# Order of VectorE in a fused attention and expert kernel: row-sum inverse and one lower half of k ahead of routing steps 7 to 12

## The reference

```python
x = x + _L0_conv_ref(_ln_c(x), mask, Wq, Wk, Wv, Wg, Wo, Wb)
#   bias = x@Wb ; sim = q.k*scale + bias ; attn = softmax(where(mask, sim, -1e9))
#   out = ((attn @ v) * sigmoid(x@Wg)) @ Wo        per row r, 160 queries x 160 keys
t = _to_tokens(x)
t = t + _L0_ffn_ref(_ln_t(t), router_w, router_b, expert_w, expert_b)
#   softmax(t@router_w + b) -> top 2 of 8, renormed ; sum of p_k * (t@expert_w[k] + expert_b[k])
```

## Time and profile before

| | |
|---|---|
| median of three runs | 909.1 us |
| profiled execution | 911.06 us |
| its span, first to last instruction | 909.2 us |
| TensorE matmul busy | 812.7 us, 89% |
| VectorE busy | 760.7 us, 84% |
| GpSimd busy | 641.0 us, 71% |
| ScalarE busy | 485.4 us, 53% |
| from 400 to 500 us | TensorE 96.31, VectorE 89.52, GpSimd 77.23, ScalarE 58.02 us of 100 |
| granted TensorE clock | 0.974 over the span, 1.00 from 400 to 500 us |

### The profile page before, as it was taken

One profiled execution on the slowest core, in us unless ns is written; L12 is line 12 of the kernel. 1 busy time (PEld: TensorE's weight loads), 2 busy tenths in 40 slices (PEclk: granted clock), 3 DMA queues, 4 the chain that ended last, 5 costly groups with the idle time before them and its releaser, 6 DMA issues.

```text
span 909.2 us, 40901 instructions
## 1 busy us (share of the span) xinstructions
PE 812.7 (89%) x15532; PEld 536.6 (59%) x15532; DVE 760.7 (84%) x1818; ACT 485.4 (53%) x1049; POOL 641.0 (71%) x1029
## 2 busy tenths in 40 slices
PE   1999678999999999999999999999999999999743
PEld 1898345656656566665666656666666666656421
DVE  8998445898898898988989989899888998898764
ACT  3886235555565555655456554555546555565410
POOL 6994002677777677776777767777677777777786
PEclk9999989999999999999999999999999999999975
DMA  4563000011110011001110011100101001100000
GB/s 126 192 197 134 19 18 25 25 31 54 39 32 30 29 50 36 29 29 34 45 36 29 29 39 40 36 29 29 45 34 36 29 29 50 36 23 25 17 14 16
DMA packets 32461, 40.82 MB, mean 45 GB/s; under 512 B 6288, under 2 KB 27280, under 8 KB 32400
## 3 DMA queue, kind: packets, MB, share of 16 engines
q1 hardware_dynamic: 31920, 39.95, 13.3%
q10 hardware_dynamic: 480, 0.02, 0.0%
HBM read 13.74 MB, written 6.55 MB: 22 GB/s over the span
## 4 chain that ended last, share of the span: by engine, by line
PE 36%; DVE 35%; issue 19%; POOL 7%; ACT 1%; DVEq 1%; DMA 0%; POOLq 0%; ACTq 0%
DVE negm L826 6%; PE psS L1113 6%; DVE rinv L842 5%; PE psS L1088 5%; DVE prod L944 3%; POOL ln_s L376 3%; PE ps_o L1170 3%; PE ps_x L1173 2%; PE ps_x L1170 2%; PE ps_o L1173 2%; DVE og L857 2%; DVE rt L906 2%; DVE q_lo L778 2%; POOL xn L379 2%; DVE ogu L849 2%
## 5 line engine op out<-in xcount | busy, mean ns | idle before, releaser
L429 POOL TENSOR_TENSOR add<-prod 128x256 f32<-128x256 f32 x160 | 116.5, 728 | 100.4 <-DVE prod L944 100.4
L826 DVE TENSOR_REDUCE negm<-psS 128x12 f16<-128x1920 f32 x80 | 146.0, 1825 | 12.8 <-PE psS L1098 7.9
L376 POOL TENSOR_TENSOR ln_s<-ln_s,half 128x5 f32<-128x5 f32 (+1 forms) x60 | 86.2, 1436 | 38.6 <-DVE ln_s L882 30.8
L434 POOL TENSOR_TENSOR add<-add 128x128 f32<-128x128 f32 x200 | 91.4, 457 | 0.1
L602 ACT ACTIVATE hl<-xn 128x320 f16<-128x320 f32 x40 | 18.8, 470 | 129.4 <-POOL xn L379 129.4
L546 ACT ACTIVATE pt_b<-psS 128x1920 f32<-128x1920 f32 x40 | 70.9, 1771 | 18.9 <-PE psS L1132 15.1
L411 POOL TENSOR_TENSOR rinv_lo<-rinv,rinv_hi 128x160 f16<-128x160 f32 x40 | 19.8, 496 | 83.8 <-ACT rinv_hi L577 83.8
L436 POOL TENSOR_TENSOR ymix<-add 128x64 f32<-128x64 f32 x200 | 64.4, 322 | 15.7
L1088 PE MATMUL psS<-bm,ident 128*128 128x480 f16 (+1 forms) x320 | 68.4, 336 | 7.0 <-ACT pt_a L546 3.1
L417 POOL TENSOR_TENSOR og_lo<-og,og_hi 128x320 f16<-128x320 f32 x80 | 61.8, 794 | 17.0 <-ACT og_hi L583 17.0
L1113 PE MATMUL psS<-bt_hi,ident 128*128 128x320 f16 (+1 forms) x320 | 68.5, 337 | 2.3 <-DVE negm L826 2.3
(11 more groups left out here) (279 smaller groups left out, 2979.5 us busy)
## 6 DMA issues: line engine op xcount, KB each, us to landing
xin<-in_x SPq DMA_DIRECT2D x20, 320.0 KB, 3.0
xs_all<-xs_pair SPq DMA_DIRECT2D x20, 320.0 KB, 2.5
xs_q<-xs_all SPq DMA_DIRECT2D x40, 160.0 KB, 2.1
xs_v<-xs_all SPq DMA_DIRECT2D x40, 160.0 KB, 2.1
xin<-in_x SPq DMA_DIRECT2D x40, 160.0 KB, 2.2
out<-res SPq DMA_DIRECT2D x40, 160.0 KB, 1.8
w_raw<-in_expert_w SPq DMA_DIRECT2D x2, 128.0 KB
eb_raw<-in_expert_b SPq DMA_DIRECT2D x15, 2.0 KB
```

The costliest lines, as they stand in the source:

```text
L376: pool.tensor_tensor(ln_s[a][:, 3, 0:w], ln_s[a][:, 2, 0:w], half[:, 0:w], ALU.pow).then_inc(own, 1)
L429: pool.tensor_tensor(add1[t % 2][:], prod_of(t)[:, 0:4, :], prod_of(t)[:, 4:8, :], ALU.add).then_inc(mix_step[t], 1)
L434: pool.tensor_tensor(add2[t % 2][:], add1[t % 2][:, 0:2, :], add1[t % 2][:, 2:4, :], ALU.add).then_inc(mix_step[t], 1)
L826: dve.tensor_reduce(negm[c][:, :, 0:slots], psS[:, :, 0:slots * N].rearrange("i h (s j) -> i h s j", s=slots), AX.X, ALU.max, negate=True) ...
```

## The change

In VectorE's step `invert(n)` moves from behind routing step 9 to behind step 6, and `qk_low(n+2, a, 1, 1, ps_o)` from behind step 12 to right behind `invert`. The third group of routing steps (7 to 9) and the fourth (10 to 12) follow both. On SyncE the hand-written walk over the steps becomes `run_steps` with a new helper that leaves out the loads of the first steps.

```diff
+        def third_on(g):
+
+            return on(g) and not (isinstance(g, int) and g < 2)
...
             def step(n, a):
                 b = 1 - a
-                if on(n + 3): load_xq(n + 3, b)
-                if isinstance(n, int) and n < 1: return
-                if on(n + 1): load_xv(n + 1, b)
+                if third_on(n + 3): load_xq(n + 3, b)
+                if third_on(n + 1): load_xv(n + 1, b)
                 if on(n - 4): store(n - 4, a)
-                if on(n + 1): load_res(n + 1, b)
-
-            for n in range(-1, LOOP):
-                step(n, n % 2)
-            pairs_loop(sp, step, LOOP, LOOP_END)
-            for n in range(LOOP_END, LAST):
-                step(n, n % 2)
+                if third_on(n + 1): load_res(n + 1, b)
+
+            run_steps(sp, step)
...
                 for k in range(4, 7):
                     if on(n - 2): route(n - 2, k)
+                if on(n): invert(n, ps_m)
+                if later(n + 2): qk_low(n + 2, a, 1, 1, ps_o)
                 for k in range(7, 10):
                     if on(n - 2): route(n - 2, k)
-                if on(n): invert(n, ps_m)
                 for k in range(10, 13):
                     if on(n - 2): route(n - 2, k)
-                if later(n + 2): qk_low(n + 2, a, 1, 1, ps_o)
```

## The result

The changed kernel takes 924.8 us (median of four runs, 923.6 to 926.8) against 909.3 us (four runs, 908.5 to 911.3). The ratio is 1.0166, with a 95% interval of 1.0151 to 1.018. The profiled execution took 923.77 us with a span of 922.0 us, 12.8 us over the span of before. The forecast was 923.1.

The account below looks back on a forecast made before the run. Bound by a ring from og through VectorE's list to L910, router_exp, exponential, q_hi, L1088 and row maximum to the next og. 36 steps x 0.39 = 14.0 us on the 909.1 us median gave 923.1 us, range 914.5 to 928.5.

Parts of the forecast that it names:

- The ring: Main loop: og, VectorE's list to L910, router_exp, exponential, q_hi, L1088, row maximum, next og set the 18.83 us period.
- The walk of steps 1 to 5: One loop step's VectorE starts, from the moved rinv through k_lo and routing steps 7 to 12: L910 0.39 us later.
- The lock: VectorE's L906 and L907 wait for GpSimd's SBUF instructions; of 0.80 us lost before, about 0.2 stay lost.
- The second rival: VectorE's L906 and L907 pass GpSimd without a wait: +0.17 us a step, 6.1 us in all, 915.2; chance 13%.
- the wait for `k_hi`: On VectorE ahead of k_lo: a new wait of 0.43 us for ScalarE's k_hi, now on the path to L910.
- the sum of strides: VectorE start-to-start changes up to L910: -0.11, +0.57 (0.43 of it the wait), +0.41, -0.29, -0.19, giving +0.39 us.
- the sign of being right: A VectorE wait of about 0.43 us ahead of k_lo, released by ScalarE's k_hi, would show the forecast right.
- The size: Main loop, n = 2 to 37: 36 steps at 0.39 us each, 14.0 us slower in all.
- within 0.1 us: Loop steps n = 38 and 39, where only invert moves: worth within 0.1 us each.
- The TensorE gap was the price: Rival: closing TensorE's 0.49 us gap ahead of project_out (L1236) gives 17.6 us, 891.5; chance 5%.
- A further slip: Rival: attention_out's bare wait, or routing instructions 9 to 12 meeting GpSimd, add 0.1 to 0.25 us: 927 to 932; 8%.
- It does nothing: Rival: a wait further on in the step absorbs both moves: 909.1, within 0.3%; chance 3%.

Follow-up runs that it names:

- e2: Only the lower half of k moved ahead of routing step 7, the inverse left behind step 9, against the kernel before: 974.2 us, ratio 1.0701.
- e1: Only the inverse moved ahead of routing step 7, the lower half of k left behind step 12, against the kernel before: 908.0 us, ratio 0.9975.
- e5: The changed kernel with GpSimd's rinv_low moved behind weigh_kept: 916.8 us, ratio 1.0076 to the kernel before.
- e3: The kernel before with the inverse ahead of routing step 7 and the lower half of k between steps 9 and 10: 919.1 us, ratio 1.01.
- e4: The changed kernel with ScalarE making k_hi ahead of keep_v and keep_m: 924.1 us, ratio 1.0153 to the kernel before.
- e7: The old VectorE order, but exponential ahead of router_exp on ScalarE and attention_out ahead of share 1 and 2 on VectorE: 916.7 us, ratio 1.0075.
- e9: Inverse alone moved, plus exponential ahead of router_exp and attention_out ahead of share 1 and 2, against the kernel before: 899.4 us, ratio 0.9882.
- e8: The changed kernel, plus exponential ahead of router_exp and attention_out ahead of share 1 and 2: 903.2 us, ratio 0.9923 to the kernel before.
- e10: Inverse moved, k between routing steps 8 and 9, exponential ahead of router_exp, attention_out ahead of share 1 and 2, against the kernel before: 890.1 us, ratio 0.9784.
- e11: Inverse ahead of routing step 7, lower half of k between steps 8 and 9, nothing else reordered, against the kernel before: 908.8 us, ratio 0.9981.
- e12: The kernel before with only SyncE's part of the change, VectorE's order as before: 910.2 us, ratio 1.0002.

## Why the prediction was right, point by point

**The ring.** Put side by side, the runs without the cut say it in one table (step 12 after `og` and period, means over the main loop; of e2 the steps at full clock):

| kernel | start of step 12 | period | difference |
|---|---|---|---|
| e1, inverse alone | 9.41 | 18.74 | 9.33 |
| before | 9.49 | 18.82 | 9.33 |
| e5, change, rinv_low later | 9.65 | 18.98 | 9.33 |
| e3, k behind step 9 | 9.70 | 19.02 | 9.32 |
| the change | 9.86 | 19.19 | 9.33 |
| e4, change, k_hi early | 9.87 | 19.19 | 9.32 |
| e2, k alone | 10.55 | 19.88 | 9.33 |

Over a range of 1.1 us the rest of the step keeps 9.33 us. "What the change does to the start of L910 is what it does to the step" is shown. With the ring cut the number is another: the difference is 9.47 us in e7, 9.08 in e9, 8.74 in e8 and 8.83 in e10.

**The walk of steps 1 to 5.** In the step at 403.35, each start after `og`, forecast and measured: `rinv` 6.54 and 6.54, `k_lo` 8.11 and 8.11, L904 8.52 and 8.52, L905 8.75 and 8.73, L906 8.98 and 8.97, step 12 9.89 and 9.89. In the neighbouring steps GpSimd is 0.04 us earlier against `og` and step 12 starts at 9.85. That parity I had not averaged: +0.37 us a step instead of +0.39.

**The lock.** L906 took 0.42 where 0.41 was forecast. The Trainium skill's rule for this (SBUF — State Buffer, "SBUF: two separate sides"), that of a VectorE instruction with two SBUF inputs and a GpSimd one the second is blocked until the first has ended, is what e4 and e5 show with VectorE as the second: 0.77 us for a 0.20 us instruction that came early, 0.20 once `rinv_lo` was elsewhere. The second rival (915.2) falls as a description of the changed kernel. Its number is nearly right for the kernel in which its condition holds, e5: 916.8.

**One attribution was wrong in kind.** In the sum I printed the wait for `k_hi`, 0.43 us, as the first term. e4 took it away and the time stayed. The walk had it right all the same, since its later lines went by the ends of `base` and `rinv_lo`; the sum of strides made it look like a price. A wait ahead of another that ends at a fixed time costs nothing. The same holds for the sign of being right that I had set on that wait: it came, and it wasn't the price.

**The size.** 36 x 0.37 = 13.3 us in the loop. From the `og` of n = 1 to that of n = 40 the profiled executions differ by more, 743.5 - 728.4 = 15.1 us: the first routing step adds 0.3, and n = 38 took 19.54 us instead of 18.04. I had put n = 38 at "within 0.1 us". The stretches in that step of the changed kernel:

```profile
855.00:858.00 3.00, 1.81 (x31) 1.35 (x34) 1.90 (x7) 1.62 (x5) 0.98 (x2) 0.91 0.19 55
858.00:861.00 3.00, 3.00 (x49) 2.50 (x40) 1.48 (x3) 0.47 (x1) 2.81 (x4) 0.52 0.02 5
```

The granted clock fell to 0.52, as in e2; in the kernel before it stayed at 1.00 in the same place. In the profiled executions it also fell there in e1, e3 and e4 (19.46 to 19.57 us), but not in e5 and e11 (17.91 and 17.92 us), although both have the earlier inverse and TensorE's idle stretches ahead of the place are the same, 1.05 and 0.81 us. So the earlier inverse doesn't bring about the fall by itself, and what decides stays open.

The start of the main part, before n = 1, came 2.2 us sooner in this execution (137.38 for 139.57), and with it the span grew by 12.8 us. The order of VectorE is the same up to there in every run but e2. Still the kernel before and e12 (139.71) lie apart from the others (136.9 to 138.7), and in those two alone four products of TensorE near 108 us (L1113, L1112 in the new code) took 1.23 us where they took 0.70 in the rest, at a granted clock of 1.00 in both; why stays open. The medians differ by 15.5 us, and the runs of one kernel lie up to 3.2 us apart. So the loop, 13.3 us where 14.0 was forecast, is what the prediction got right. That the two profiled executions lie 12.7 us apart, so near to 14.0, is in part luck: effects at both ends of the main part, +1.5 and -2.2 us, stood in no term and nearly cancel.

**The rivals.** "The TensorE gap was the price" falls with e1. The advice that I had set beside it (Trainium skill, Perfetto Trace Analysis, "Optimization Strategy": close the gaps of the most-contended engine) gave 2 us while the gap was slack and 17 with the ring cut, counted from e7. "A further slip" did not happen: `attention_out` started at 10.70 us, 0.31 later than before, and L1087 still went by the exponential. "It does nothing" did not happen.

## To carry to other kernels

Before moving an instruction up, find which start keeps a constant distance to the next period, in two neighbouring steps that differ a little, and count what the move does to that start; a gap on the busiest engine that fails this test is slack. An instruction that waits for another engine should go where its input is just ready and its own engine would be blocked anyway; two routing steps further up cost 15 us here, one further down 9, that position nothing. And a short instruction that waits for a long chain shouldn't stand in a queue ahead of one that the next period depends on: exchanging them gave 8.6 to 21.6 us in the three orders with the earlier inverse, but cost 6.6 us in the old order, where the instruction put back was now the one waited for.

## What the runs showed of the hardware that I had not expected

- TensorE's granted clock fell to 1.2 GHz inside the loop behind an idle stretch of 1.75 us and stayed at 2.4 behind one of 1.55 us in the next step (e2), but four steps kept it behind 1.73 to 1.76 us and one lost it behind 1.57. A step with such a fall was 1.4 us longer.
- A VectorE instruction on 40 elements a partition with two inputs in SBUF took 0.20 us alone and 0.77 to 0.79 behind GpSimd, ending 0.05 to 0.07 us after it (e1, e4), while `k_lo` and the inverse, with an input in PSUM, kept their times beside the same GpSimd instructions (0.42 to 0.50 and 1.14 us).
- In the middle of the loop, without the cut and at full clock, L1087's weight load kept 1.74 to 1.77 us to the start of the exponential, however much else had moved.
